# Gram with nine matmuls per group: low parts of the diagonal blocks in their lower triangles, rows divided by the diagonal, VectorE alone makes the diagonal block

## The chip, the cores and the metric

One NeuronCore of a Trainium2 chip runs the kernel. The time is the device time in microseconds (us) of one launch; the median of several executions counts. One more execution was profiled, and all rows below come from it.

## What is computed

For each of B=8 batches: S=112 query rows of width C=320, 20 heads of 16; a context of 375 rows of width 512, of which 371 (`text`) and 4 (`ip`) are attended apart. Cut to what matters:

```python
q = heads(x @ W_q); k_t = heads(text @ W_k); v_t = heads(text @ W_v)
probs_t  = softmax(q . k_t / 4)                       # over the 371 text rows
text_out = probs_t . v_t
qsem  = l2norm(probs_t . text)                        # 512 wide, for each head and query row
fused = q . k_ip / 4 + 0.5 * (qsem . l2norm(ip))      # 4 columns
out   = (text_out + softmax(fused) * mask . v_ip) @ W_out + b_out + x
```

The norm of `probs_t . text` is not taken from 512 wide vectors. With e the unnormalised probabilities and G = text . text^T (371x371, symmetric), its square is e^T G e. G is kept in two rounded parts, a high one (`Gh`) and the remainder (`Gl`), so that fast matmuls (type f32r) can use it.

## The kernel before

**Tiling.** The 371 text rows are three chunks (`ROWS`: 128, 128, 115). Heads go in groups of four: NG=5 groups per batch, g = 0 to 39 in all. For each group:

- `St` (S0, S1, S2, one per chunk): four matmuls of 112 columns into one of two PSUM banks `P`. ScalarE (ACT) takes the exponential into `big` (`eb`, line 681), then rounds it into `er` (line 685).
- `gram`, for j = 2, 1, 0: sums over i <= j of block (i, j) of G times chunk i of `er`, into one of two banks `Y`. Blocks above the diagonal carry a factor 2, so the upper triangle suffices. Each block takes two matmuls of 448 columns, one with `Gh` and one with `Gl`: 6 + 4 + 2 = 12. VectorE (DVE) multiplies each Y by `eb` (line 829) and GpSimd (POOL) adds the three products (line 547). `gram(g, 2)` waits for all three `er` of its group (`s_er`), and gram number y for the product of gram y-2 (`s_P`), since there are two banks `Y`.
- `pv` (v): 12 matmuls with V and 4 that add the products; ACT copies the result to `OT`.

**Preparation of a batch**, one batch ahead, shares three PSUM banks `PR` (the ring, NR=3): units `K` (keys: ACT rounds, DVE takes the rest), `G` (a block row of G, i = 0, 1, 2), `V`, 20 `max` (m: scores of one head, DVE reduces to the maximum, line 807), `mT` (transposes the maxima after the last m), and of the batch before `T`, `pT`, `cT`, `o`. A unit that writes ring bank n waits until the unit n-3 has been freed by its last reader (`freed`).

A unit `G` before: 12 matmuls into the bank; ACT copies the diagonal block to `Gh` (line 658), then twice the rest (line 661), then four columns to `Vt` (line 665); DVE writes both parts of `Gl` (lines 799, 801) and frees the bank.

**Order.** Each engine runs its instructions in the order of one list (`master_schedule`). For group g = 5b + r the words of `ROUNDS[r]` (batches 1 to 6), `EARLY[r]` (batch 0) or `LAST[r]` (batch 7) are written out one after the other. In them g stands for gram(g, 2), gram(g, 1), gram(g, 0); S0 to S2 for the St of group g+1; v for pv of group g-1; K, Kr for batch b+2; m, G, V, mT for batch b+1; T, r, pw, z, p, pT, cT, o for the end of batch b-1. ACT follows the list exactly; DVE follows it too, except that `behind()` lets some work wait until a later unit. `LATE` replaces the last round of batches 5 and 6.

Of the kernel before, what the change touches and what calls it, by code (L numbers as in the profile page):

```python
# [50 lines left out]
ROUNDS = ("S0 K0 m g m K1 S1 m v S2 m G0 m",  # L51
# [17 lines left out]
def master_schedule():  # L69
# [14 lines left out]
    order += [("G", 0, i) for i in range(3)] + [("K", 1, c) for c in range(3)] + [("Kr", 1)]  # L84
# [70 lines left out]
def build(nc, xT, xr, ctxT, ctxip, mask, wq, wk, wv, wkip, wvip, wout, bout, ident_d, hm_q, hm_v, krow, out):  # L155
# [13 lines left out]
    with ctx:  # L169
        def sb(name, shape, dt=f32):  # L170
            return ctx.enter_context(nc.sbuf_tensor(name, shape, dt))

# [16 lines left out]
        Gl = [sb(f"Gl{i}", [128, 768], f32r) for i in range(2)]  # L189
# [298 lines left out]
        def _(pool):  # L488
            fills = [0]

            def fill(region, value):
# [14 lines left out]
            fill(usel[:, 21:22], 1.0)  # L506
# [104 lines left out]
        def _(act):  # L611
# [3 lines left out]
            for u in order:  # L615
# [34 lines left out]
                elif k == "G":  # L650
                    b, i, r = u[1], u[2], ROWS[u[2]]
                    filled(act, u)
# [22 lines left out]
                elif k == "St":  # L675
# [9 lines left out]
                    act.activation(er[g % 2][:, 448 * c:448 * c + 448], e, ACT.Copy).then_inc(s_er, 1)  # L685
# [46 lines left out]
        def _(dve):  # L732
# [8 lines left out]
            for u in behind(order):  # L741
# [48 lines left out]
                elif k == "G":  # L790
                    b, i, r = u[1], u[2], ROWS[u[2]]
                    if b == 0:
                        dve.wait_ge(s_set, FILLS)
                    dve.wait_ge(s_gh, 3 * b + i + 1)
                    gh, gl = Gh[b % 2], Gl[b % 2]
                    a = min(128, T - 128 * i)
                    rest = T - 128 * i - a
                    o = GOFF[i]
                    low = dve.tensor_tensor(gl[0:r, o:o + a], bank[0:r, 0:a], gh[0:r, o:o + a].bitcast(f32), ALU.subtract)
                    if rest:  # L800
                        low = dve.scalar_tensor_tensor(gl[0:r, o + a:o + a + rest], bank[0:r, a:a + rest], 2.0,
                                                       gh[0:r, o + a:o + a + rest].bitcast(f32), ALU.mult, ALU.subtract)
# [100 lines left out]
        def _(pe):  # L903
# [6 lines left out]
            for u in order:  # L910
# [57 lines left out]
                elif k == "G":  # L968
# [8 lines left out]
                    last.then_inc(s_ring, 1)  # L977
                elif k == "V":
# [16 lines left out]
                elif k == "mT":  # L995
                    b = u[1]
                    if b == 0:
                        pe.wait_ge(s_w, 16 * FIRST)
# [18 lines left out]
                elif k == "gram":  # L1017
# [5 lines left out]
                    if j == 2 and r == 0:  # L1023
                        freed(pe, seq[("G", b, 2)])
# [149 lines left out]
```

## Time and profile before

| | |
|---|---|
| median of 3 executions | 411.6 us (411.37 to 414.6) |
| the profiled execution | 411.41 us, its span 409.6 us |
| TensorE (PE) matmuls | 393.6 us busy, 96% of the span |
| VectorE, ScalarE, GpSimd | 54%, 50%, 50% |

A row of a timeline gives start and duration in us, engine, line and operation, out<-in, shape and count, and in brackets how long the engine had been idle and who ended that. Durations of matmuls overlap: what a matmul costs the engine is the distance between two starts. PEld is the load of a matmul's weights. A row with x2 or more is several alike merged. Line numbers of these rows are those of the kernel before.

### The profile page before, as it was taken

The page shows a single profiled execution, that of the slowest core. Times are in us where ns is not written, and L with a number is a line of the kernel's source. Part 1 is how long each engine was busy: PE and PEld are TensorE (multiplying, and loading weights), DVE is VectorE, ACT ScalarE, POOL GpSimd, SP SyncE. Part 2 cuts the span into 40 slices and gives each one's busy share as a digit, 9 for nine tenths or more (in the row PEclk, how much of TensorE's full clock was granted, in tenths as well). Part 3 has the DMA queues.
Part 4 walks back from the last instruction along what each step waited for, and adds up shares of the span by engine and source line. Part 5 has one row for each costly group of instructions (what it writes and reads, how often), then busy time and mean ns, then how long its engine had stood idle before and what let it go on. Part 6 is the DMA issues. An engine that isn't in the chain of part 4 may idle for free.

```text
span 409.6 us, 9494 instructions
## 1 busy us (share of the span) xinstructions
PE 393.6 (96%) x3653; PEld 319.5 (78%) x3653; DVE 220.2 (54%) x482; ACT 206.0 (50%) x484; POOL 206.3 (50%) x218
## 2 busy tenths in 40 slices
PE   7999799899899999999999999999999999999995
PEld 4648688678788878888789878887888878876762
DVE  0795764575267534665366526663556646643432
ACT  1534134555645565555556564456455366458722
POOL 3020361262527872576437662687247443844981
PEclk9999999999999999999999999999999999999998
DMA  8499994338204802273207511470208210001000
GB/s 259 140 292 234 213 172 84 92 126 166 75 2 150 145 14 72 75 161 61 82 6 193 97 49 36 146 144 18 72 2 168 51 40 2 3 3 39 3 16 15
DMA packets 29455, 38.03 MB, mean 93 GB/s; under 512 B 14361, under 2 KB 26745, under 8 KB 28729
## 3 DMA queue, kind: packets, MB, share of 16 engines
q1 hardware_dynamic: 28514, 36.36, 37.0%
q10 hardware_dynamic: 896, 1.07, 0.9%
q8 instruction: 29, 0.48, 0.5%
q14 instruction: 16, 0.13, 0.1%
HBM read 28.50 MB, written 8.81 MB: 91 GB/s over the span
## 4 chain that ended last, share of the span: by engine, by line
PE 88%; DVE 3%; ACT 2%; issue 2%; DMA 2%; POOL 1%; POOLq 0%; SPq 0%; ACTq 0%; DVEq 0%
PE PR L905 42%; PE Y L905 27%; PE P L905 10%; PE O L905 8%; DMA pb<-wq 1%; DVE big L773 1%; PE PR L1063 1%; ACT big L681 1%; ACT er L685 1%; POOL pb L547 1%; DVE mx L807 1%; DMA qst<-ma 0%; POOLq L169 0%; SPq L460 0%; ACT cTs L729 0%
## 5 line engine op out<-in xcount | busy, mean ns | idle before, releaser
L547 POOL TENSOR_TENSOR pb<-pb 128x448 f32<-128x448 f32 x78 | 89.1, 1142 | 110.4 <-DVE pb L829 104.9
L807 DVE TENSOR_REDUCE mx<-PR 112x1 f32<-112x371 f32 x160 | 83.7, 540 | 78.1 <-PE PR L905 77.1
L905 PE MATMUL Y<-er,Gh 128*128 128x448 f32 x240 | 95.3, 397 | 1.7 <-ACT er L685 0.8
L829 DVE TENSOR_TENSOR pb<-big,Y 128x448 f32<-128x448 f32 x120 | 72.6, 621 | 39.2 <-PE Y L905 39.0
L905 PE MATMUL Y<-er,Gl 128*128 128x448 f32 x240 | 87.3, 364 | 0.0
L681 ACT ACTIVATE big<-P 128x448 f32<-128x448 f32 x120 | 65.2, 543 | 18.7 <-PE P L905 17.9
L685 ACT ACTIVATE er<-big 128x448 fp32r<-128x448 f32 x120 | 69.3, 578 | 3.8
L905 PEld LDWEIGHTS Y<-er,Gh 128*128 128x128 f32 x240 | 45.1, 188 | 13.7 <-DVE pb L829 9.1
L905 PE MATMUL PR<-kst,qst 96*112 96x371 bf16 x160 | 51.3, 331 | 2.2 <-DVE mx L807 2.0
L905 PEld LDWEIGHTS Y<-er,Gl 128*128 128x128 f32 x240 | 45.2, 188 | 2.1
L905 PE MATMUL P<-qst,kst 99*128 99x112 bf16 x480 | 42.0, 214 | 1.5 <-ACT big L681 1.1
L905 PEld LDWEIGHTS P<-qst,kst 99*128 99x128 bf16 x480 | 29.8, 99 | 17.0 <-issue 8.0
L649 ACT ACTIVATE ks<-PR 128x372 bf16<-128x372 f32 (+1 forms) x24 | 10.3, 429 | 47.8 <-PE PR L905 47.2
L905 PE MATMUL PR<-wvh,eh 128*128 128x320 f32 (+1 forms) x96 | 32.3, 336 | 0.2 <-ACT Vt L673 0.2
L673 ACT ACTIVATE Vt<-PR 128x320 f32<-128x320 f32 (+1 forms) x24 | 10.6, 442 | 41.2 <-PE PR L905 41.2
L905 PE MATMUL O<-big,Vt 128*22 128x112 f32 x960 | 31.0, 262 | 0.0
L905 PE MATMUL PR<-eh 128*128 128x376 f32 (+2 forms) x96 | 29.7, 310 | 0.0
L905 PE MATMUL PR<-wvl,eh 128*128 128x320 f32 (+1 forms) x96 | 29.7, 309 | 0.0
L905 PE MATMUL PR<-wvh,el 128*128 128x320 f32 (+1 forms) x96 | 29.6, 309 | 0.0
L569 POOL TENSOR_TENSOR t<-ssq,halfm 112x20 f32<-112x20 f32 (+2 forms) x9 | 28.8, 3202 | 1.4 <-DVE ssq L845 1.3
L905 PE MATMUL PR<-eh,el 128*128 128x376 f32 (+2 forms) x96 | 28.0, 292 | 0.0
L905 PE MATMUL PR<-el,eh 128*128 128x376 f32 (+2 forms) x96 | 28.0, 292 | 0.0
(154 smaller groups left out, 653.5 us busy)
## 6 DMA issues: line engine op xcount, KB each, us to landing
et<-ctxT SPq DMA_DIRECT2D x8, 752.0 KB, 4.4
kst<-kd SPq DMA_DIRECT2D x7, 720.0 KB, 7.2
kd<-ks SPq DMA_DIRECT2D x16, 288.0 KB, 2.9
qst<-qd SPq DMA_DIRECT2D x48, 70.0 KB, 2.4
kst<-kd SPq DMA_DIRECT2D x7, 480.0 KB, 9.9
kst<-kd SPq DMA_DIRECT2D x9, 240.0 KB, 9.0
qd<-kst SPq DMA_DIRECT2D x4, 336.0 KB, 5.6
vx<-xr SPq DMA_DIRECT2D x8, 140.0 KB, 2.2
```

The source lines that it names most:

```text
L547: pool.tensor_tensor(total, total, (pz, pm)[j], ALU.add).then_inc(s_S, 1)
L569: power = pool.tensor_tensor(t1[:, hs], ssq[:, hs], halfm[:, hs], ALU.pow)
L649: act.activation(ks[:, 0, TP * c:TP * c + w], bank[:, 0:w], ACT.Copy).then_inc(s_kh, 1)
L673: act.activation(Vt[b % 2][0:r, i, :, 0:D], bank[0:r, 0:C].rearrange("p (h d) -> p h d", d=D), ACT.Copy).then_inc(s_free[seq[u] % NR], 1)
L681: act.activation(e, P[(3 * g + c) % 2][:, 0:448], ACT.Exp).then_inc(s_exp, 1)
L685: act.activation(er[g % 2][:, 448 * c:448 * c + 448], e, ACT.Copy).then_inc(s_er, 1)
L773: dve.tensor_tensor(kblk[0:w, c, :, :].rearrange("p b (h n) -> p b h n", n=NIP), src, m, ALU.mult).then_inc(s_kb, 1)
L807: dve.tensor_reduce(mx[b % 2][:, h:h + 1], bank[0:S, 0:T], AX.X, ALU.max).then_inc(s_free[seq[u] % NR], 1)
L829: dve.tensor_tensor((pz, pm, pa[g % 2])[j], eb[g % 3][:, 448 * j:448 * j + 448], Y[y % 2][:, 0:448], ALU.mult).then_inc(s_P, 1)
L905: return pe.matmul(o, st, mv, start=start, stop=stop, **kw)
L1063: last = pe.transpose(bank[0:S, 128 * (r - lo):128 * (r - lo) + 128], OT[b % 2][:, r, :], ident[:, :])
```

## The change

- `er` is now the exponential times a number per text row (`gc`, the diagonal of G), rounded; the rows of G are divided by that number (`grc` its reciprocal) when they are copied. The diagonal of the divided block is exactly 1.
- The diagonal block of `Gh` holds, above the diagonal, the rounded values and half the diagonal; below it, the transposed low parts. So one matmul per diagonal block does what two did: gram takes 5 + 3 + 1 = 9 matmuls. The result is half of what it was; `usel` carries 2.0.
- DVE makes the diagonal block: six instructions per unit `G`, each waiting for the one before. ACT waits for the fifth (`s_gd`), then copies the rest and the `Vt` columns; DVE's part for the rest (`Gl`) comes as a held unit after the next max.
- A new ring unit `D` per block row: PE transposes the 128x128 low parts, and DVE adds them into `Gh`.
- The lists are rewritten: where G and D stand, and where m, K and V stand around them.

```diff
-ROUNDS = ("S0 K0 m g m K1 S1 m v S2 m G0 m",
-          "S0 m g m K2 m S1 v m S2 G1 m",
-          "S0 m g2 T0 T1 g1 g0 m r0 G2 m S1 m pw v S2 m V0",
-          "Kr S0 r1 m g m V1 m S1 m m v r2 S2 mT z V2",
+ROUNDS = ("S0 K0 m K1 m g m G0 S1 m v S2 m",
+          "S0 g m D0 m K2 m G1 S1 m v S2 m",
+          "S0 g2 T0 T1 g1 g0 m D1 r0 m G2 S1 m v S2 m pw",
+          "Kr S0 r1 g m D2 V0 m S1 m V1 m v r2 m S2 m mT z V2",
           "p E g pT v cT S0 S1 o S2")
 EARLY = ("m S0 m K1 g m S1 m S2 m",
-         "S0 m g m S1 K2 m S2 v m m",
-         "S0 m g m S1 m v S2 V0 m m",
-         "Kr S0 m g m V1 m S1 m m v S2 mT V2",
+         "S0 m D0 g m S1 K2 m S2 v m m",
+         "S0 m D1 g m S1 m v S2 V0 m m",
+         "Kr S0 m D2 g m V1 m S1 m m v S2 mT V2",
...
-    order += [("G", 0, i) for i in range(3)] + [("K", 1, c) for c in range(3)] + [("Kr", 1)]
+    order += [("G", 0, i) for i in range(3)]
+    order += [u for c in range(3) for u in (("K", 1, c), ("D", 0, c))] + [("Kr", 1)]
...
 ACT, unit G:
-                    filled(act, u)
+                    act.wait_ge(s_gd, 3 * b + i + 1)
...
-                    act.activation(Gh[b % 2][0:r, GOFF[i]:GOFF[i] + a], bank[0:r, 0:a], ACT.Copy)
-                    rest = T - 128 * i - a
+                    rest = T - 128 * i - r
                     if rest:
...
+                        act.activation(Gh[b % 2][0:r, GOFF[i] + r:GOFF[i] + r + rest], bank[0:r, r:r + rest],
+                                       ACT.Copy, scale=grc[b % 2][0:r, i:i + 1])
 ACT, unit St:
-                    act.activation(er[g % 2][:, 448 * c:448 * c + 448], e, ACT.Copy).then_inc(s_er, 1)
+                    act.activation(er[g % 2][:, 448 * c:448 * c + 448], e, ACT.Copy,
+                                   scale=gc[g // NG % 2][:, c:c + 1]).then_inc(s_er, 1)
 DVE, unit G:
+                    link(dve.scalar_tensor_tensor(low, bank[0:r, 0:r], 1.0, ident[0:r, 0:r], ALU.mult, ALU.mult, accum_out=c))
+                    link(dve.tensor_scalar(c, c, TINY, None, ALU.max))
+                    link(dve.reciprocal(rc, c))
+                    link(dve.scalar_tensor_tensor(diag, bank[0:r, 0:r], rc, half_upper[0:r, 0:r], ALU.mult, ALU.mult))
+                    dve.scalar_tensor_tensor(low, bank[0:r, 0:r], rc, diag.bitcast(f32), ALU.mult, ALU.subtract).then_inc(s_gd, 1)
+                    dve.wait_ge(s_gd, 3 * b + i + 1)
+                    dve.scalar_tensor_tensor(low, low, c, upper[0:r, 0:r], ALU.mult, ALU.mult).then_inc(s_ru, 1)
 DVE, units Gl and D (new):
+                        dve.scalar_tensor_tensor(Gl[b % 2][0:r, LOFF[i]:LOFF[i] + rest], PR[n % NR][0:r, r:r + rest],
+                                                 grc[b % 2][0:r, i:i + 1], Gh[b % 2][0:r, o + r:o + r + rest].bitcast(f32),
+                                                 ALU.mult, ALU.subtract).then_inc(s_free[n % NR], 1)
+                    dve.scalar_tensor_tensor(diag, bank[0:r, 0:r], grc[b % 2][0:r, i:i + 1], diag.bitcast(f32), ALU.mult,
+                                             ALU.add).then_inc(s_free[seq[u] % NR], 1)
 PE, units D (new) and gram:
+                    pe.wait_ge(s_ru, 3 * b + i + 1)
+                    pe.transpose(bank[0:r, 0:r], dj[i][0:r, 0:r], ident[0:r, 0:r]).then_inc(s_ring, 1)
...
-                        mm(d, Gh[b % 2][:, o:o + 128], mv, i == 0, False)
-                        last = mm(d, Gl[b % 2][:, o:o + 128], mv, False, i == j)
+                        last = mm(d, Gh[b % 2][:, o:o + 128], mv, i == 0, i == j)
+                        if i < j:
+                            o = LOFF[i] + 128 * (j - i - 1)
+                            mm(d, Gl[b % 2][:, o:o + 128], mv, False, False)
```

PE, from S2 of a round 0 (batch 2) to the first gram matmul of round 1. `P1<-qst2,kst2` is S2, `P0<-qst2,kst2` the next S0, `PR..<-kst0,qst0` a max, `PR2<-eh1`, `el1` the unit G0. Before:

```order
L905 MATMUL P1<-qst2,kst2 128x112 x4
L905 MATMUL PR1<-kst0,qst0 112x371
L905 MATMUL PR2<-eh1 128x376
L905 MATMUL PR2<-el1,eh1 128x376
L905 MATMUL PR2<-eh1,el1 128x376
...
L905 MATMUL PR0<-kst0,qst0 112x371
L905 MATMUL P0<-qst2,kst2 128x112 x4
L905 MATMUL PR1<-kst0,qst0 112x371
L905 MATMUL Y1<-er1,Gh0 128x448
```

and in the changed kernel, the end of G0 and what follows it:

```order
L941 MATMUL PR1<-eh1,el1 128x376
L941 MATMUL P0<-qst2,kst2 128x112 x4
L941 MATMUL PR2<-kst0,qst0 112x371
L941 MATMUL O<-big,Vt1 22x112 x12
L941 MATMUL O<-pb,usel 22x112 x4
L941 MATMUL P1<-qst2,kst2 128x112 x4
L941 MATMUL PR0<-kst0,qst0 112x371
L941 MATMUL P0<-qst2,kst2 128x112 x4
L941 MATMUL Y1<-er1,Gh0 128x448
```

G0 stood between S2 and the gram; it now stands ahead of S1, and one max and the next S0 are left between S2 and the gram. Rounds 1 and 2 changed in the same way around G1 and G2.

ACT, at the same place. `big<-P` is the exponential of an St, `er` its rounding, `Gh`, `Vt` the copies of unit G. Before:

```order
L681 ACTIVATE big<-P0 128x448
L685 ACTIVATE er1<-big 128x448
L693 ACTIVATE OT1<-O 128x112
L681 ACTIVATE big<-P1 128x448
L685 ACTIVATE er1<-big 128x448
L658 ACTIVATE Gh1<-PR2 128x128
L661 ACTIVATE Gh1<-PR2 128x243
L665 ACTIVATE Vt1<-PR2 128x20x4
```

and in the changed kernel:

```order
L676 ACTIVATE Gh1<-PR1,grc1 128x243
L680 ACTIVATE Vt1<-PR1 128x20x4
L696 ACTIVATE big<-P0 128x448
L700 ACTIVATE er1<-big,gc0 128x448
L709 ACTIVATE OT1<-O 128x112
L696 ACTIVATE big<-P1 128x448
L700 ACTIVATE er1<-big,gc0 128x448
```

G's copies stood behind the er of S2; they now stand ahead of the exponential of S1.

PE, behind the gram of a round 1 (the last two gram matmuls, then max, D0, max, K2, whose first matmul is the last row). Before:

```order
L905 MATMUL Y1<-er1,Gh0 128x448
L905 MATMUL Y1<-er1,Gl0 128x448
L905 MATMUL PR2<-kst0,qst0 112x371
L905 MATMUL PR0<-et,wk2 64x186 x8
L905 MATMUL PR1<-kst0,qst0 112x371
```

and in the changed kernel:

```order
L941 MATMUL Y1<-er1,Gh0 128x448
L941 MATMUL PR1<-kst0,qst0 112x371
L1019 MATMUL PR2<-masks,dj0 128x128
L941 MATMUL PR0<-kst0,qst0 112x371
L941 MATMUL PR1<-et,wk2 64x186 x8
```

The unit three places behind the first max was a max behind K2; it is now K2 itself, with only D0 and one max between.

## Rows read from the trace of the kernel before

**Rows 1.** The page: busy time of PE; the chain that ended last, by engine.

```profile
PE 393.6 (96%) x3653; PEld 319.5 (78%) x3653; DVE 220.2 (54%) x482; ACT 206.0 (50%) x484; POOL 206.3 (50%) x218
...
PE 88%; DVE 3%; ACT 2%; issue 2%; DMA 2%; POOL 1%; POOLq 0%; SPq 0%; ACTq 0%; DVEq 0%
```

**Rows 2.** Windows: stretch, length, busy us of PE, PEld, DVE, ACT, POOL, then PEclk.

```profile
120.00:320.00 200.00, 199.23 (x1964) 168.57 (x1962) 109.84 (x246) 108.16 (x257) 118.55 (x115) 1.00 0.38 89
...
402.00:406.00 4.00, 3.14 (x10) 1.12 (x10) 1.58 (x8) 1.33 (x5) 0.76 (x1) 1.00 0.00 0
```

**Rows 3.** Timeline, PE: last matmuls of a gram (g = 11) and the max behind it.

```profile
211.38 0.36 PE L905 MATMUL Y<-er,Gl 128*128 128x448 f32 x1
211.66 0.47 PE L905 MATMUL Y<-er,Gh 128*128 128x448 f32 x1
211.97 0.36 PE L905 MATMUL Y<-er,Gl 128*128 128x448 f32 x1
212.17 0.32 PE L905 MATMUL PR<-kst,qst 96*112 96x371 bf16 x1
```

**Rows 4.** Timeline, PE: S1; S2 behind max and pv; max, S0, max behind G0.

```profile
205.21 0.37 PE L905 MATMUL P<-qst,kst 99*128 99x112 bf16 x4
...
206.57 0.37 PE L905 MATMUL P<-qst,kst 99*128 99x112 bf16 x4
...
209.05 0.32 PE L905 MATMUL PR<-kst,qst 96*112 96x371 bf16 x1
209.21 0.36 PE L905 MATMUL P<-qst,kst 99*128 99x112 bf16 x4
209.41 0.32 PE L905 MATMUL PR<-kst,qst 96*112 96x371 bf16 x1
```

**Rows 5.** Timeline, ACT: the same stretch.

```profile
206.35 0.58 ACT L685 ACTIVATE er<-big 128x448 fp32r<-128x448 f32 x1
206.84 0.24 ACT L693 ACTIVATE OT<-O 128x112 f32<-128x112 f32 x1
206.98 0.54 ACT L681 ACTIVATE big<-P 128x448 f32<-128x448 f32 x1
...
209.43 0.37 ACT L661 ACTIVATE Gh<-PR 128x243 fp32r<-128x243 f32 x1
...
209.80 0.57 ACT L681 ACTIVATE big<-P 128x448 f32<-128x448 f32 x1
210.40 0.58 ACT L685 ACTIVATE er<-big 128x448 fp32r<-128x448 f32 x1
```

**Rows 6.** Timeline, batch 0: an S2, its er, the gram that waits for it.

```profile
79.09 0.37 PE L905 MATMUL P<-qst,kst 99*128 99x112 bf16 x4
...
80.10 0.58 ACT L685 ACTIVATE er<-big 128x448 fp32r<-128x448 f32 x1
...
80.83 0.44 PE L905 MATMUL Y<-er,Gh 128*128 128x448 f32 x1 [0.84 <-ACT er L685]
```

**Rows 7.** Timeline, DVE: two small instructions, the second waiting for the first.

```profile
404.25 0.20 DVE L860 RECIPROCAL zm<-zm 112x8 f32<-112x8 f32 x1
404.49 0.23 DVE L861 TENSOR_SCALAR zm<-zm,mask_s 112x8 f32<-112x8 f32 x1
```

**Rows 8.** Timeline, DVE: the maximum of the max that PE starts at 212.17.

```profile
212.91 0.54 DVE L807 TENSOR_REDUCE mx<-PR 112x1 f32<-112x371 f32 x1
```

**Rows 9.** Timeline, PE: transposes of 128 columns.

```profile
174.14 0.71 PE L1063 MATMUL PR<-ident,OT 128*112 128x128 f32 x5
```

**Rows 10.** Timeline: the two places before group 0 with three units G together.

```profile
37.51 0.28 DVE L799 TENSOR_TENSOR Gl<-PR,Gh 128x128 fp32r<-128x128 f32 x1
...
38.45 0.39 PE L905 MATMUL PR<-eh,wkh 128*128 128x372 f32 x1
...
66.26 0.28 ACT L658 ACTIVATE Gh<-PR 128x128 fp32r<-128x128 f32 x1 [3.12 <-PE PR L905]
...
69.42 0.54 ACT L681 ACTIVATE big<-P 128x448 f32<-128x448 f32 x1 [0.21 <-PE P L905]
```

More of the change, by code:

```diff
@@ L21 @@
 GOFF = (0, 384, 640)
+LOFF = (0, 256)
+TINY = 1e-30
 STACK = ((0, 3), (1, 2), (2, 1))
-FILLS = 17
-FIRST, REST = 2, 6
+FILLS = 19
+FIRST, REST = 1, 6
 HH = 10
@@ L101, in master_schedule @@
                 unit.update({"G0": ("G", n, 0), "G1": ("G", n, 1), "G2": ("G", n, 2)})
+            if n < B:
+                unit.update({"D0": ("D", n, 0), "D1": ("D", n, 1), "D2": ("D", n, 2)})
             if n + 1 < B:
@@ L135, in behind @@
     for u in order:
-        if u[0] in ("K", "G") and u[1] >= 2:
+        if u[0] == "K" and u[1] >= 2:
             out, held = out + held, [u]
+        elif u[0] == "G":
+            out, held = out + held + [u], [("Gl",) + u[1:]]
         else:
             out.append(u)
-            if u[0] in ("max", "gram", "mT", "o"):
+            if u[0] in ("max", "gram", "mT", "o", "K"):
                 out, held = out + held, []
     return out + held
-RING = ("K", "G", "V", "T", "pT", "cT", "o", "max", "mT")
+RING = ("K", "G", "D", "V", "T", "pT", "cT", "o", "max", "mT")
 NR = 3
@@ L188, in build @@
         Gh = [sb(f"Gh{i}", [128, 768], f32r) for i in range(2)]
-        Gl = [sb(f"Gl{i}", [128, 768], f32r) for i in range(2)]
+        Gl = [sb(f"Gl{i}", [128, 384], f32r) for i in range(2)]
+        gc = [sb(f"gc{i}", [128, 3]) for i in range(2)]
+        grc = [sb(f"grc{i}", [128, 3]) for i in range(2)]
+        dj = [sb(f"dj{i}", [128, 128]) for i in range(3)]
         Vt = [sb(f"Vt{i}", [128, 3, H, MV]) for i in range(2)]
@@ L225, in build @@
         res = [sb(f"res{i}", [S, C]) for i in range(2)]
+        ident, half_upper, upper = [masks[:, 128 * i:128 * i + 128] for i in range(3)]
         vrT = et[:, 0, 0:H * NIP * 3].rearrange("p (c n) -> p c n", c=3)
@@ L256, in build @@
         s_w2 = sem("s_w2")
+        s_mk = sem("s_mk")
         s_pw = sem("s_pw")
@@ L287, in build @@
         s_pad = sem("s_pad")
+        s_gd = sem("s_gd")
         s_gh = sem("s_gh")
+        s_ru = sem("s_ru")
         s_ms = sem("s_ms")
@@ L505, in _ @@
             fill(usel[:, :], 0.0)
-            fill(usel[:, 21:22], 1.0)
+            fill(usel[:, 21:22], 2.0)
+            for i in range(2):
+                fill(gc[i][:, :], 1.0)
             fill(half[:, :], 0.5)
@@ L977, in _ @@
                     last.then_inc(s_ring, 1)
+                elif k == "D":
+                    b, i, r = u[1], u[2], ROWS[u[2]]
+                    pe.wait_ge(s_ru, 3 * b + i + 1)
+                    if b == 0 and i == 0:
+                        pe.wait_ge(s_mk, 16)
+                    pe.transpose(bank[0:r, 0:r], dj[i][0:r, 0:r], ident[0:r, 0:r]).then_inc(s_ring, 1)
                 elif k == "V":
@@ L1023, in _ @@
                     if j == 2 and r == 0:
-                        freed(pe, seq[("G", b, 2)])
+                        for i in range(3):
+                            freed(pe, seq[("D", b, i)])
                     if j == 2:
@@ L1163 @@
         "bout": np.ascontiguousarray(L0_xattn_b_out),
-        "ident_d": np.eye(128, dtype=np.float32),
+        "ident_d": np.concatenate([np.eye(128), np.triu(np.ones((128, 128)), 1) + np.eye(128) / 2,
+                                   np.triu(np.ones((128, 128)), 1)], 1).astype(np.float32),
         "hm_q": np.ascontiguousarray(hm_q),
```

33 lines of the change are left out of this document (20 added, 13 removed).

## The prediction

> **What bounds the kernel now.** I read the page first. TensorE is busy for 96% of the span and makes 88% of the chain of work that ended last [rows 1]; from 120 to 320 us it is busy for 199.2 of 200 us [rows 2]. Matmul durations overlap, so I went by the distance between starts. A gram matmul costs 0.20 us (211.97 to 212.17) [rows 3]. Steady batches run with PE nearly gapless. So work taken from PE shortens the kernel, but only while nothing that PE waits for becomes late. I therefore read next, in the timeline, how long the others need from a trigger on PE to the thing PE wants back, and compared it with the work that stands between the two in PE's order, now and in the change.
>
> **What the change removes.** Three of twelve matmuls in each of 40 groups: 120 x 0.20 = 24.0 us.
>
> **What gram gives back at once.** gram j=0 waits for DVE's product of j=2, with only the matmuls of j=1 to cover it. Now this costs 0.28 - 0.20 = 0.08 us in the start (211.38 to 211.66) and 0.11 more behind it (0.31 to the next instead of 0.20) [rows 3]. The cover shrinks from four matmuls to three, so the wait grows by one matmul, 0.20 us. That holds for the 29 groups whose list says g (5 in batch 0, 24 in batches 1 to 6), and about for four groups of the last batch: 33 x 0.20 = 6.6 us.
>
> **D on PE.** Five transposes together last 0.71 us [rows 9], so one costs at most 0.14 us: 24 x 0.14 = 3.4 us.
>
> **ACT behind the diagonal chain: the largest term.** gram(g, 2) needs the er of its group's S2. In batch 0 there is one place where almost nothing stands between: S2 starts at 79.09, its er at 80.10, gram at 80.83, after PE had idled 0.84 us [rows 6]. So S2 to gram takes 1.74 us with ACT free. In the steady rounds before, S2 to the max ahead of gram is 206.57 to 209.41 = 2.84 us, since G0 (or G1, V) stood between [rows 4]. In the new rounds 0, 1 and 2 only a max and the next S0 follow S2: 0.20 + 0.16 + 0.20 = 0.56 us of PE work [rows 4]. That alone leaves PE 1.74 - 0.56 = 1.18 us idle. And ACT won't be free: in its order the copies of G stand ahead of S1's exponential, and they now wait for DVE.
>
> Take 0 as the end of G0's slots on PE. Its bank is full at +0.20 (a matmul ends 0.16 after the next may start [rows 3], plus 0.04 to hand over). DVE then runs five instructions, each waiting for the one before: two like the 128x128 subtraction of 0.28 [rows 10], reading PSUM, a maximum and a reciprocal on one column, and another 128x128. Dependent small ones stand 0.24 apart at 0.20 each, so 0.04 is the handover [rows 7]. That is 3 x 0.29 + 2 x 0.20 + 4 x 0.03 = 1.39 us. The trace has no instruction with an accumulator output: it may cost nothing, or one more small instruction (0.24); I take nothing. From below the chain is 1.27 (no handovers), from above 1.39 + 0.24 + 0.2 (small ones as long as the second of rows 7, wider ones slower) = 1.83. ACT starts at +1.65. From there its distances are the measured ones [rows 5]: copy to exponential 0.37 (209.43 to 209.80), exponential to er 0.60, er to OT 0.49, OT to exponential 0.14, exponential to er again 0.60, so S2's er starts at +3.85; from start of er to gram is 0.73 (80.10 to 80.83) [rows 6]: gram at +4.58. PE meanwhile has S1, max, pv (1.36, 205.21 to 206.57), S2, max, S0 (0.56) [rows 4] = 1.92 us. **PE idles 2.66 us.** Around G1 the copy is shorter by 0.10: 2.56. Around G2 there is no rest to copy and the block is 115 wide: 2.36. Per batch 7.58, in six batches 45.5 us. Queued behind ACT's wait are the exponentials of S1 and S2, for which PE's next S0 and the gram wait; nothing on PE can step ahead, since it runs in order.
>
> The scale of er is a column of numbers now; whether this costs ACT anything no row shows. I take nothing, and for the upper end 0.1 us in each of eight such instructions on the way (two er and mostly a copy per stall): 4.8 us.
>
> The Trainium skill ("ScalarE: Activation LUTs", section "What ACT_TABLE_LOAD costs") says that each pointer operand of an ACTIVATE adds about 93 ns. By it the sum below would be 8 x 6 x 0.093 = 4.5 us higher (an estimate from that page); the trace of before has no such ACTIVATE.
>
> **The ring.** A unit waits until the one three places ahead is freed. Behind the gram of round 1 stand max, D0, max, K2; K2 waits for the first max. PE starts a max at 212.17, DVE reaches it at 212.91 because it multiplies products first, and frees it 0.54 later [rows 3, 8]: 1.28 + 0.06 = 1.34 us. PE has 0.16 + 0.14 + 0.16 = 0.46 us of work: 0.88 idle. Round 2 has max, D1, max, G2 behind g1 g0, where with g1 and g0 next to each other both products still lie ahead of DVE (I take 0.4 us more, two matmuls less of head start): 1.29. In round 3 mT now follows a max at once and waits for it: three maxima in a row at 0.5 apart with S2 between, 0.9. Together 3.07, in six batches 18.4 us. Twice in batch 0 D waits 0.3: 0.6 us. From below all of this could be nothing, if DVE frees sooner.
>
> **Before group 0.** Two places have three units G together. DVE takes them strictly in turn: chain 1.39, ACT 0.05 + 0.5, Gl 0.44, so about 2.4, 2.3, then 1.4 to the third's release. At the second place the bank is full at 66.26 and the first exponential ran at 69.42 [rows 10]; now it can't before 66.26 + 2.4 + 2.3 + 1.4 + 0.1 = 72.5, and the ring holds K: I take 2.5 us (of up to 3.1). At the first place DVE starts at 37.51 and K at 38.45 [rows 10]; K now waits to 37.5 + 2.4 = 39.9 (1.4), the next K for the third G (2.8 more): 4.2. Together 6.7, from below nothing.
>
> **Sum.** -24.0 + 6.6 + 3.4 + 45.5 + 18.4 + 0.6 + 6.7 = +57.2. On the profiled execution's 411.4 this gives 468.6; the median is 0.2 higher: **469 us**. The extra DVE work (about 1.4 us per G, 34 us in all, on an engine busy 54%) costs nothing beyond the chain. If only the ring term falls away the time is 450; with the chain at 1.83 (18 x 0.44 = 8) and er dearer (4.8) it is 482; a few waits of the V copies that I left out add 2 or 3. Own range: 446 to 488.
>
> **Rivals.**
> - *The chain doesn't hold ACT* (ACT finds the diagonal done, or the copies overlap): each stall is only the 1.18 us of S2 to gram. 18 x 1.18 = 21.2 instead of 45.5: 444 us. For it: rows 6 show that figure; against it: the chain is bounded from below by 1.27 us.
> - *Faster:* PE's work decides, as it does now [rows 1, 2], and the stalls don't come: -24.0 + 6.6 + 3.4 = -14.0, 397 us. It needs er(S2) within 0.56 us of S2, or stalls and ring waits below 14.0 / 18 = 0.78 us per round. Rows 6 show 1.74, so I hold little of it. The Trainium skill ("Perfetto Trace Analysis", "Identifying Performance Opportunities") speaks for this one: it says that improving a kernel means improving its most contended engine, here PE, which the change relieves.
> - *No change:* the stalls come to about 14 us by luck: 411 us.
> - *The clock falls:* PE now idles 2.5 us at a time. Where it already idles some 0.9 us in 4, the granted clock stayed at 1.00 [rows 2], its level of 2.4 GHz; longer gaps no row shows. If PE ran half of the 6.3 us it streams per stalled round at 1.2 GHz, that is 3.1 x 18 = 56 us more: about 525 us. The Trainium skill ("TensorE: Matmul & The Clock Gate", "What's actually happening") says that the throttled state is the default, and activity releases it.
>
> **How the numbers follow.** Forecast 0.72; chain doesn't hold ACT 0.12; clock 0.07; faster 0.06; no change 0.03. Forecast and first rival together fill 442 to 490, with a little cut off each end. Faster by over 1% 0.06, within 1% (about what a measurement of this kernel can tell) 0.03, slower by over 1% 0.91.
>
> **What would show it.** In steady batches, three gram matmuls per batch with 2.4 to 2.7 us idle before them, released by er; the ACT copy of G waiting for DVE's fifth instruction, 1.4 us after the first; K2, G2 and mT waiting for a maximum by 0.9 to 1.3 us; PE busy near 80% of the span with its clock at 1.00; gram matmuls still 0.20 apart; a steady batch longer by 7.6 + 3.1 - 3.0 + 0.8 + 0.4 = 8.9 us. The prediction is wrong if gram's idle time in these rounds is below 1 us, if the DVE chain takes under 1 us, or if the clock drops.

## The result and the profile after

| | before | after |
|---|---|---|
| median | 412.2 us (4 runs, 411.4 to 414.6) | 501.7 us (4 runs, 500.6 to 503.7) |
| ratio | | 1.217 (1.210 to 1.223) |
| span of the profiled execution | 409.6 us | 499.1 us |
| mean granted clock of TensorE | 0.997 | 0.934 |
| a steady batch, from one transpose of the maxima (mT) to the next, mean of four | 44.6 us | 58.2 us |

The kernel is 89.6 us slower. Forecast was 57 slower, and the time lies above the range. The page of the changed kernel: busy time, the clock in 40 slices, the chain that ended last.

```profile
PE 413.6 (83%) x3557; PEld 322.6 (65%) x3557; DVE 259.5 (52%) x650; ACT 210.1 (42%) x460; POOL 205.9 (41%) x220
...
PEclk9998998999878998889988998889969998999998
...
PE 56%; DVE 17%; ACT 10%; issue 9%; POOL 4%; DMA 2%; SPq 1%; POOLq 0%; ACTq 0%; DVEq 0%
```

Against [rows 1] PE fell from 96 to 83% busy, and DVE and ACT entered the chain. PE is busy for longer although it has 96 matmuls less: the clock row dips all through the kernel. The waits (engine and what it waited for: us in total, times, longest):

```profile
ACT Gh L676 <- DVE dj L820: 68.8, 16, 7.4
ACT Vt L680 <- DVE dj L820: 33.5, 8, 5.2
PE Y L941 <- ACT er L700: 31.3, 20, 1.7
PE P L941 <- ACT big L696: 17.5, 22, 1.5
PEld PR L941 <- DVE mx L843: 16.8, 15, 1.4
PEld Y L941 <- DVE pb L865: 14.3, 32, 1.4
PE PR L1043 <- DVE mx L843: 5.7, 7, 0.8
```

These are the waits that the prediction named: ACT stands for DVE's fifth instruction, gram for er, K2, G2 and mT for a maximum. The fourth row is the next S0, which waits for the exponential of S1, since that frees its bank P; it was named too. A steady round 0, first DVE's chain for one G, then ACT behind it:

```profile
186.42 0.29 DVE L816 SCALAR_TENSOR_TENSOR dj<-PR,masks 128x128 f32<-128x128 f32 x1 [1.23 <-PE PR L941]
186.63 0.08 DVE L816 DVE_READ_ACCUMULATOR dj<-PR,masks 128x1 f32 x1
186.75 0.15 DVE L817 TENSOR_SCALAR gc<-gc 128x1 f32<-128x1 f32 x1
186.94 0.16 DVE L818 RECIPROCAL grc<-gc 128x1 f32<-128x1 f32 x1
187.14 0.35 DVE L819 SCALAR_TENSOR_TENSOR Gh<-PR,grc,masks 128x128 fp32r<-128x128 f32 x1
187.53 0.35 DVE L820 SCALAR_TENSOR_TENSOR dj<-PR,grc,Gh 128x128 f32<-128x128 f32 x1
```

```profile
187.91 0.46 ACT L676 ACTIVATE Gh<-PR,grc 128x243 fp32r<-128x243 f32 x1 [5.89 <-DVE dj L820]
188.27 0.23 ACT L680 ACTIVATE Vt<-PR 128x80 f32<-128x80 f32 x1
188.39 0.55 ACT L696 ACTIVATE big<-P 128x448 f32<-128x448 f32 x1
188.97 0.67 ACT L700 ACTIVATE er<-big,gc 128x448 fp32r<-128x448 f32 x1
...
190.25 0.67 ACT L700 ACTIVATE er<-big,gc 128x448 fp32r<-128x448 f32 x1
```

and PE: S2, max, the next S0, then gram(g, 2):

```profile
187.51 0.37 PE L941 MATMUL P<-qst,kst 99*128 99x112 bf16 x4
187.71 0.32 PE L941 MATMUL PR<-kst,qst 96*112 96x371 bf16 x1
188.99 0.37 PE L941 MATMUL P<-qst,kst 99*128 99x112 bf16 x4 [0.95 <-ACT big L696]
191.06 0.71 PE L941 MATMUL Y<-er,Gh 128*128 128x448 f32 x1 [1.70 <-ACT er L700]
191.57 0.57 PE L941 MATMUL Y<-er,Gl 128*128 128x448 f32 x1
191.95 0.57 PE L941 MATMUL Y<-er,Gh 128*128 128x448 f32 x1
```

PE is idle for 0.95 + 1.70 = 2.65 us; by starts it is (1.28 - 0.16) + (2.07 - 0.20) = 2.99. Behind it the gram matmuls start 0.37 to 0.38 apart instead of 0.20. Windows of the same place (stretch, length, PE busy, granted clock, DMA) say why:

```profile
190.00:191.00 1.00, 0.00 (x0) 0.98 0.00 0
191.00:192.00 1.00, 0.94 (x3) 0.50 0.06 16
192.00:193.00 1.00, 1.00 (x4) 0.50 0.00 0
...
194.00:195.00 1.00, 1.00 (x6) 0.81 0.00 0
```

At the end of the stall the clock falls from 1.00 to 0.50, its level of 1.2 GHz, for some 3 us of dense work. The stalls of the next two rounds do the same (0.50 again from 205 to 208 and from 215 to 218 us). But not every stall does. Taken in windows of 1 us, the clock fell after 13 of the 18, and stayed at 1.00 after those that end at 273.75, 380.69, 390.59, 431.64 and 441.54 us. The first of these five, with the next matmul close behind:

```profile
273.75 0.44 PE L941 MATMUL Y<-er,Gh 128*128 128x448 f32 x1 [1.70 <-ACT er L700]
274.03 0.37 PE L941 MATMUL Y<-er,Gl 128*128 128x448 f32 x1
```

Over the whole span, 499.1 x (1 - 0.934) = 33 us of clock is lost, against 1 before.

### The profile page after: what moved, and what is told of

The parts are those of the page before. It is cut to its first block, busy times and chain, and to the rows that moved or that the text cites. A ratio compares the mean times of both kernels' runs of the same rounds, so it can differ in the third digit from the quotient of the medians.

```text
span 499.1 us, 9507 instructions
## 1 busy us (share of the span) xinstructions
PE 413.6 (83%) x3557; PEld 322.6 (65%) x3557; DVE 259.5 (52%) x650; ACT 210.1 (42%) x460; POOL 205.9 (41%) x220
## 3 DMA queue, kind: packets, MB, share of 16 engines
q10 hardware_dynamic: 896, 1.07, 0.7%
## 4 chain that ended last, share of the span: by engine, by line
PE 56%; DVE 17%; ACT 10%; issue 9%; POOL 4%; DMA 2%; SPq 1%; POOLq 0%; ACTq 0%; DVEq 0%
PE PR L941 32%; PE Y L941 15%; DVE pb L865 4%; ACT big L696 4%; PE P L941 4%; DVE mx L843 3%; ACT er L700 3%; PE O L941 3%; DMA et<-ctxT 2%; DVE Gh L819 2%; DVE dj L820 2%; POOL pb L564 2%; DVE dj L816 1%; POOL t L586 1%; PE PR L1109 1%
## 5 line engine op out<-in xcount | busy, mean ns | idle before, releaser
L941 PE MATMUL Y<-er,Gh 128*128 128x448 f32 x240 | 98.3, 444 | 35.4 <-ACT er L700 31.3
L865 DVE TENSOR_TENSOR pb<-big,Y 128x448 f32<-128x448 f32 x120 | 71.5, 619 | 90.8 <-PE Y L941 88.7
L843 DVE TENSOR_REDUCE mx<-PR 112x1 f32<-112x371 f32 x160 | 82.5, 536 | 53.2 <-PE PR L941 52.9
L941 PEld LDWEIGHTS Y<-er,Gh 128*128 128x128 f32 x240 | 53.1, 221 | 52.8 <-issue 34.4
L700 ACT ACTIVATE er<-big,gc 128x448 fp32r<-128x448 f32 x120 | 80.3, 669 | 3.9
L941 PE MATMUL P<-qst,kst 99*128 99x112 bf16 x480 | 42.2, 214 | 18.4 <-ACT big L696 17.5
L941 PE MATMUL PR<-kst,qst 96*112 96x371 bf16 x160 | 52.5, 341 | 2.5 <-DVE mx L843 2.4
L941 PEld LDWEIGHTS P<-qst,kst 99*128 99x128 bf16 x480 | 27.4, 98 | 36.1 <-ACT big L696 23.4
L941 PE MATMUL Y<-er,Gl 128*128 128x448 f32 x120 | 50.4, 420 | 0.0
L676 ACT ACTIVATE Gh<-PR,grc 128x243 fp32r<-128x243 f32 (+1 forms) x16 | 6.6, 410 | 68.8 <-DVE dj L820 68.8
L941 PE MATMUL PR<-eh 128*128 128x376 f32 (+2 forms) x96 | 30.8, 321 | 5.4 <-DVE mx L843 5.4
```

The source lines that it names most:

```text
L676: act.activation(Gh[b % 2][0:r, GOFF[i] + r:GOFF[i] + r + rest], bank[0:r, r:r + rest], ACT.Copy, scale=grc[b % 2][0:r, i:i + 1])
L843: dve.tensor_reduce(mx[b % 2][:, h:h + 1], bank[0:S, 0:T], AX.X, ALU.max).then_inc(s_free[seq[u] % NR], 1)
L865: dve.tensor_tensor((pz, pm, pa[g % 2])[j], eb[g % 3][:, 448 * j:448 * j + 448], Y[y % 2][:, 0:448], ALU.mult).then_inc(s_P, 1)
L941: return pe.matmul(o, st, mv, start=start, stop=stop, **kw)
```

## The experiments

"Clock lost" is the span times one minus the mean granted clock, of the profiled execution. Batch is the steady batch as above.

| kernel | median us | ratio to before | clock lost | batch |
|---|---|---|---|---|
| after | 501.7 | 1.217 (1.210 to 1.223) | 32.9 | 58.2 |
| e1 order alone | 453.3 | 1.097 (1.091 to 1.102) | 8.5 | 51.0 |
| e2 8 idle matmuls | 481.2 | 1.164 (1.157 to 1.170) | 10.1 | 54.6 |
| e2b 4 idle matmuls | 482.0 | 1.166 (1.161 to 1.171) | 8.2 | 54.9 |
| e3 copies late | 451.4 | 1.092 (1.087 to 1.098) | 4.9 | 49.9 |
| e4 old lists | 438.4 | 1.061 (1.056 to 1.067) | 9.2 | 47.6 |
| e5 e3 and ring | 447.8 | 1.085 (1.080 to 1.090) | 4.5 | 49.3 |
| e6 er by a constant | 495.2 | 1.198 (1.194 to 1.202) | 29.1 | 57.3 |
| e7 new lists | 423.2 | 1.025 (1.020 to 1.030) | 7.1 | 44.0 |
| e8 and batch 0 | 417.3 | 1.011 (1.002 to 1.019) | 2.1 | 44.0 |
| e9 and nip moved | 416.2 | 1.006 (1.004 to 1.009) | 4.1 | 44.0 |
| e10 and start | 418.5 | 1.014 (1.011 to 1.017) | 7.1 | 44.0 |

**e1: the order alone, without the new arithmetic.** The kernel before, with the new `ROUNDS` less their D. Here and in the diffs below `...` marks a cut.

```diff
-ROUNDS = ("S0 K0 m g m K1 S1 m v S2 m G0 m",
-          "S0 m g m K2 m S1 v m S2 G1 m",
+ROUNDS = ("S0 K0 m K1 m g m G0 S1 m v S2 m",
+          "S0 g m m K2 m G1 S1 m v S2 m",
...
```

> The kernel before with the changed kernel's ROUNDS (without the D units), arithmetic as before: twelve matmuls per gram, no chain on VectorE. Theory (the places in the list are a cause by themselves): S2 to gram(g,2) takes 1.74 us with ScalarE free and the list leaves 0.56 us of work between, so TensorE idles about 1.2 us in rounds 1, 2 and 3 of six batches (21 us), and the ring waits of K2, G2 and mT (0.9, 1.3, 0.9) stay (18 us): 411.6 + 39 = about 451 us, if the granted clock stays at 1.00. If gaps of 1.2 us already make the clock fall, 1.5 us more for each of 18: about 478 us, mean clock near 0.94. Rival (the chain on VectorE is the whole cause): within 5 us of 412.

453.3 us, near the 451 that the theory gave. Twelve matmuls, ACT making the diagonal block, and still 41 us slower: gram waits for er 19 times.

```profile
PE Y L905 <- ACT er L685: 22.1, 19, 1.5
```

So nearly half of the loss is there before DVE's chain enters: too little work stands between S2 and gram, and between a maximum and the unit that takes its bank. The clock fell after 3 of the 18 stalls (1.52 us long; it stayed after three others of 1.52, and after all those of 1.05 and 0.97).

**e2 and e2b: keep PE awake.** The changed kernel with idle matmuls (results unused) ahead of gram(g, 2)'s wait in rounds 1 to 3 of batches 1 to 6. They are 448 columns wide, 0.20 us each; the 128 in the text of e2b is wrong.

```diff
+                    if j == 2 and 1 <= b < B - 1 and 1 <= r <= 3:
+                        for _ in range(FILL):
+                            mm(d, Gh[b % 2][:, 0:128], Gh[b % 2][:, 0:448], True, True)
                     if j == 2:
                         pe.wait_ge(s_er, 3 * g + 3)
```

> The changed kernel with eight more matmuls of 448 columns (Gh times Gh, into the bank Y that gram overwrites, so the output is the same) ahead of the wait for er in rounds 1, 2, 3 of batches 1 to 6: 144 matmuls more, in the 1.7 us in which TensorE idles. Theory (the part of the loss that the prediction missed is the clock, which falls to 0.50 after each of these 18 stalls and costs about 1.6 us each): mean granted clock 0.99 or more, gram matmuls 0.20 us apart behind the wait, time 501.7 - 29 = about 473 us (468 to 478). Rival (the miss is longer waits, the low clock only goes along): no gain, or slower by the added work, 500 to 510 us.

> e2_filler with 4 idle products of 128 columns instead of 8 ahead of the gram product that waits for er; the products go nowhere, the computation is complete. Theory (the clock falls after long idle stretches of TensorE; e3's of 1.1 us left it at 1.00, the changed kernel's of 1.7 behind 1.2 did not): 4 fill some 0.25 us or more of the 1.7, which is between the two: about 481 us if the clock then stays as in e2_filler, about 500 us if it falls as in the changed kernel.

481.2 and 482.0 us. Matmuls that compute nothing make the kernel 20.6 us faster. They stand where PE would have idled, and what they buy is the clock: 200 us of steady batches, after, with 8 and with 4 of them (PEclk is the number behind the five engines):

```profile
150.00:350.00 200.00, 163.44 (x1492) 132.61 (x1492) 99.33 (x257) 85.05 (x187) 92.52 (x91) 0.92 0.27 63
```

```profile
150.00:350.00 200.00, 179.63 (x1668) 144.97 (x1666) 105.23 (x271) 90.87 (x198) 95.61 (x93) 1.00 0.29 68
```

```profile
150.00:350.00 200.00, 172.97 (x1623) 138.13 (x1622) 104.29 (x268) 89.99 (x196) 95.09 (x93) 0.99 0.28 66
```

The clock fell after none of the 18 stalls with eight, and after two of them with four (0.58 from 143 to 147 and 0.57 from 188 to 192 us). Filling about half of the 1.7 us (with 0.8 still waited for er) serves nearly as well as filling all. The waits of S0 for ACT are the same in e2 as after (17.5 us, 22 times). This prices the clock: 20.6 us by the medians, 32.9 - 10.1 = 23 by the clock itself, and a batch of 58.2 against 54.6.

**e3: ACT doesn't wait for the chain.** ACT's copies of G, from batch 2 on, stand behind the er of S2 in ACT's list; PE and DVE are as after. The new function, cut to what matters:

```diff
+        if u[0] == "G" and 2 <= u[1]:
+            held = [u]
+        else:
+            out.append(u)
+            if u[0] == "St" and u[2] == 2:
+                out, held = out + held, []
```

> The changed kernel, only ScalarE's order changed: its copies of G (from batch 2 on) stand behind the er of S2 instead of ahead of S1's exponential, so that no exponential waits for VectorE's chain. Theory: the wait of the next S0 (0.6 to 0.9 us and more) goes, and gram's wait shrinks to that of S2's er, about 1.3 us with an er of 0.67; stalls of 2.9 us become 1.3 us: 18 x 1.6 = 29 us less, 473 us if the clock still falls after each, 445 us with a mean clock of 0.99 if it doesn't. Rival (ScalarE's wait for the chain is not on the path): 495 to 503 us.

451.4 us, 50 less. S2 and the gram of the same round, with what it still waits:

```profile
187.09 0.37 PE L954 MATMUL P<-qst,kst 99*128 99x112 bf16 x4
...
188.89 0.45 PE L954 MATMUL Y<-er,Gh 128*128 128x448 f32 x1 [1.07 <-ACT er L713]
189.17 0.36 PE L954 MATMUL Y<-er,Gl 128*128 128x448 f32 x1
```

S2 to gram is 187.09 to 188.89 = 1.80 us, near the 1.74 that the prediction took from [rows 6]. The matmuls behind stay 0.2 apart: none of the 18 stalls of 1.07 us was followed by a lower clock. Against e2 (481.2 us, the clock back and the waits kept) e3 is 29.8 us shorter, and the theory had 29 for the waiting; the other 20.6 of the 50 us are the clock, as e2 priced it. So the branch of the theory in which the clock no longer falls (445 us) is the one that came, 6 us too low. Its stalls were to be 1.3 us; they are 1.07 by the bracket and 1.23 by starts (187.46 for S0, 188.89 for gram).

**e4: the new arithmetic in the old order.** Before's lists, with D put in.

```diff
+ROUNDS = ("S0 K0 m g m K1 S1 m v S2 m G0 m",
+          "S0 m g m D0 K2 m S1 v m S2 G1 m",
+          "S0 m g2 T0 T1 g1 g0 m D1 r0 G2 m S1 m pw v S2 m V0",
+          "Kr S0 r1 m g m D2 V1 m S1 m m v r2 S2 mT z V2",
...
```

> The changed kernel's arithmetic (nine matmuls, chain on VectorE, D) with the lists of before for batches 1 to 6, the D units put in behind the gram of rounds 1 and 3 and behind the max of round 2. Theory: G0, G1 and V stand between S2 and gram again, so er is never late, the clock stays at 1.00, and what is left is 24.0 us saved against 6.6 (gram j=0), 3 (D), 6 to 7 before group 0, and waits of T0 for G1's bank, about 1 us in six batches: 400 to 412 us. Rival (the arithmetic itself is what costs, wherever it stands): over 440 us.

438.4 us: 63 us won, but neither the 400 to 412 expected nor over 440, though close under the rival's bound. er is in time now; other waits took its place, the longest for DVE's products.

```profile
PEld Y L941 <- DVE pb L865: 26.4, 32, 2.2
PE Y L941 <- DVE pb L865: 12.9, 12, 1.8
```

G stands next ahead of gram in these lists, so its chain and its Gl lie in DVE's order ahead of the products that gram's own last part waits for: the chain starts at 175.74, Gl at 178.07, the products at 178.90. Once a batch gram waits 1.7 to 1.8 us for them, and T 1.2 us for the bank of G1, which the theory had named. After three of the six long waits for the products the clock fell. One of them:

```profile
179.56 0.47 PE L941 MATMUL Y<-er,Gh 128*128 128x448 f32 x1 [1.80 <-DVE pb L865]
```

**e5: free the ring.** e3, with other work between the maxima and K2, G2 and mT.

```diff
-          "S0 g m D0 m K2 m G1 S1 m v S2 m",
+          "S0 g m D0 K2 m m G1 S1 m v S2 m",
...
```

> e3_copies_late (451.42 us) with the lists of rounds 1 to 3 written so that at least one product or S2 stands between each D or G and the r, K or V that takes the next of the ring of tiles. Theory (the ring term): the waits for VectorE's max before K2 (0.9 to 1.3 us), G2 (1.3) and mT (0.9), some 3 us a batch in six batches, go: 18 us less, about 433 us. Rival (the waits only uncover another wait behind them, on er or on the block's factor): 448 us or more.

447.8 us, only 3.6 less, with intervals that overlap; the rival held. In a timeline of PE, K2 waits no more (0.73 us in e3), but G1, three places behind it, waits 0.79 us for K2's own bank. G2 waits no more either (1.07 in e3), but the third max behind it does, for G2's bank:

```profile
197.19 0.36 PE L954 MATMUL PR<-kst,qst 96*112 96x371 bf16 x1 [1.52 <-DVEq L846]
```

DVE frees that bank (line 846) only behind ACT's copies of G2, which e3 had moved behind the er of S2. So the wait for a maximum went, and another wait for a bank of the ring came, with the units three places behind the moved ones.

**e6: the price of the column.** er's scale is a constant; the multiplication of er by `gc` is left out.

```diff
-                                   scale=gc[g // NG % 2][:, c:c + 1]).then_inc(s_er, 1)
+                    act.activation(er[g % 2][:, 448 * c:448 * c + 448], e, ACT.Copy).then_inc(s_er, 1)
```

> The changed kernel with a constant in place of the column gc as scale of the activation that writes er, so the multiplication of er by gc is left out. Theory (the column costs 0.09 us an activation, 669 against 577 ns in the two traces, and counts where ScalarE is what TensorE waits for, twice a round in 18 rounds): 2 x 0.09 x 18 = 3.3 us less, 498.5 us. Rival (the row difference comes from something else, or ScalarE's time there is hidden): no change, 501.7 us.

495.2 us, 6.6 less instead of 3.3. er of the changed kernel and of e6 in the groups of instructions (busy us, mean ns):

```profile
L700 ACT ACTIVATE er<-big,gc 128x448 fp32r<-128x448 f32 x120 | 80.3, 669 | 3.9
```

```profile
L700 ACT ACTIVATE er<-big 128x448 fp32r<-128x448 f32 x120 | 69.3, 577 | 3.8
```

92 ns an instruction. The wait of gram for er is 1.52 us here instead of 1.70, and 18 x 0.18 = 3.2 us is what the theory had. The rest goes with the clock (32.9 - 29.1 = 3.8 us lost less): here it fell after 14 of the 18 stalls, for the same 3 us each time; in the changed kernel after 13, but from 133 to 140 and from 365 to 376 us it stayed low two and three times as long. Whether the shorter stalls have a part in that isn't shown.

**e7: lists for this arithmetic.** A K or V stands between S2 and gram, every G a round ahead, a max between g2 and g1, and ACT's copies behind the next S.

```diff
+ROUNDS = ("S0 K0 m m g2 m g1 g0 S1 m v m G0 S2 K1 m",
+          "S0 m g2 m g1 g0 D0 S1 m v m G1 S2 K2 m",
+          "S0 g2 T0 T1 g1 g0 m D1 r0 S1 m pw v m G2 S2 V0 m",
+          "Kr S0 r1 m g2 m g1 g0 D2 V1 m S1 m m v r2 S2 mT z V2",
...
```

> The arithmetic with nine matmuls a group, complete, with ScalarE's copies of a block held behind the next S's exponential, lists in which a K or V product stands between S2 and the gram product of the same round, every G a round ahead of the group that uses it, and other products between the gram products of one group. Theory (all the loss is of order, and the nine matmuls save 120 x 0.20 = 24 us of TensorE): 393 to 400 us, the granted clock at 1.00 in the steady batches. Rival (VectorE's chain of six small instructions for a block costs TensorE time wherever it stands): 425 us or more.

423.2 us: 78.5 us of the 89.6 came back by order alone, with the arithmetic untouched, though not the 393 to 400 expected, and with little left to the rival's 425. The same place as above (end of G, S2, first matmul of K1; its last, max, S0, max, gram):

```profile
217.80 0.34 PE L953 MATMUL PR<-eh,el 128*128 128x376 f32 x1
217.97 0.37 PE L953 MATMUL P<-qst,kst 99*128 99x112 bf16 x4
218.16 0.42 PE L953 MATMUL PR<-eh,wkh 128*128 128x372 f32 x1
...
220.13 0.34 PE L953 MATMUL PR<-eh,wkl 128*128 128x372 f32 x1
220.30 0.32 PE L953 MATMUL PR<-kst,qst 96*112 96x371 bf16 x1
220.46 0.36 PE L953 MATMUL P<-qst,kst 99*128 99x112 bf16 x4
220.90 0.36 PE L953 MATMUL PR<-kst,qst 96*112 96x371 bf16 x1
221.00 0.47 PE L953 MATMUL Y<-er,Gh 128*128 128x448 f32 x1
```

No wait: 2.14 us of K1 cover er and the chain, which takes as long as ever (218.25 to 219.71 on DVE). A batch is 44.0 us, 0.6 less than before. The nine matmuls promised 3.0. In the timelines of one batch each, the starts of the gram matmuls span 13.4 us for 60 before and 11.4 for 45 here, so 2.0 is the true gain; a gram matmul that follows another unit takes 0.3 instead of 0.2, and splitting a group into pieces makes more of these. D (0.4) and short waits around S and max take back about 1 more. The other loss lies in batch 0 and the next, where clock falls follow waits.

**e8, e9, e10: batch 0.** e8 puts D behind the group's products; e9 moves three instructions of DVE on `nip` (2.25 us, once) to a calmer place; e10 puts K and G ahead of the first S.

```diff
-         "S0 m D0 g m S1 K2 m S2 v G2 m m",
+         "S0 m g D0 m S1 m K2 v S2 G2 m",
...
+                    if u == ("max", 1, 19):
+                        dve.tensor_scalar(nip[:, :], nip[:, :], EPS, None, ALU.max).then_inc(s_nip, 1)
...
-    order += [("mT", 0), ("G", 1, 0)] + [("St", 0, 0), ("St", 0, 1), ("K", 2, 0), ("St", 0, 2)]
+    order += [("mT", 0), ("G", 1, 0), ("K", 2, 0), ("G", 1, 1)] + [("St", 0, c) for c in range(3)]
```

> e7_new_lists with the lists of batch 0 changed so that the products of a group stand ahead of the D that needs VectorE's chain, and a pv product stands between K2 and the G behind it. In e7 TensorE stood 2.12 us ahead of a D at 85.6 us and 1.52 us ahead of a max product at 94.7 us, and the granted clock was 0.50 from 95 to 98 us behind it. Theory (these waits are of order): 2.1 + 1.5 us of waiting and some 1.5 us of low clock go, about 418 us. Rival (the chain moves the wait to the next product): 422 us or more.

> e8_early with VectorE's three instructions on nip (2.25 us in a row, once) moved from between the products of group 7 to behind the last max of batch 1. In e7 they stood ahead of a max for which TensorE waited 1.73 us at 142.0 us, and the granted clock was 0.50 from 143 to 149 us. Theory (this single delay starts the fall of the clock): 1.7 us of waiting and 3.5 us of low clock go against e8, about 413 us. Rival (something else makes the clock fall there): as e8.

> e9_early_nip with the first K product of batch 2 and the second G of batch 1 moved ahead of the first S, where TensorE stood 2.77 us for the DMA of the maxima and the granted clock was 0.50 from 71 to 77 us. Theory (that wait is covered by 3.4 us of products, and the fall of the clock behind it goes too): 2.8 us of waiting and some 3 us of low clock less than e9's 416.2, about 411 us, 2 us below before. Rival (the ring of tiles holds the moved products back, or the DMA's wait isn't shortened): 414 us or more.

417.3 (expected 418), 416.2 (expected 413; the rival, as e8, held) and 418.5 us (expected 411; the rival's 414 or more held). In e9 the wait at 142 us is gone, and so is the fall of the clock there. But in e8's profile that same wait was there, and the clock stayed. The wait in e7 and the window behind it (stretch, length, PE busy, granted clock), then the same of e8:

```profile
142.04 0.36 PE L953 MATMUL PR<-kst,qst 96*112 96x371 bf16 x1 [1.73 <-DVE mx L855]
...
144.00:148.00 4.00, 4.00 (x19) 0.50 0.84 154
```

```profile
139.71 0.36 PE L953 MATMUL PR<-kst,qst 96*112 96x371 bf16 x1 [1.74 <-DVE mx L855]
...
138.00:148.00 10.00, 8.29 (x59) 1.00 0.84 174
```

So a single stall of 1.7 us doesn't decide it, and what sets it stays open. The order of the program doesn't decide it either: of four launches of e8 two had a mean clock of 0.995 and 0.999 (415.5 and 414.4 us) and two of 0.983 (419.2 and 419.9 us). In e10 the wait for the DMA of the maxima went as planned, but the first S2 then stood behind an ACT that waited for the chain of the second G, the very pattern of the change:

```profile
78.01 0.36 ACT L688 ACTIVATE Gh<-PR,grc 128x115 fp32r<-128x115 f32 x1 [2.60 <-DVE dj L832]
```

```profile
78.98 0.55 PE L953 MATMUL P<-qst,kst 99*128 99x112 bf16 x4 [2.65 <-ACT big L708]
```

No version beat the kernel before: the best, e9, is 0.6% slower (0.4 to 0.9).

## Why the prediction was right and wrong

**Right: the mechanism and its places.** All three stalled rounds, ACT held by the chain, K2, G2 and mT held by a maximum, each in the row that was named. The rival "faster" fails on [rows 6], as said: gram needs 1.7 to 1.8 us from S2. The rule of the Trainium skill that stood beside it ("Perfetto Trace Analysis", "Identifying Performance Opportunities"), to improve the most contended engine, doesn't hold by itself here: PE was relieved of 24 us of matmuls, and the order took 78.5 (e7).

**The terms, one by one.**
- *The stall behind the chain*, forecast 2.66 us, was 2.99 by starts in round 0. DVE starts 0.27 behind the end of G0's slots (forecast 0.20), and its chain to ACT took 187.91 - 186.42 = 1.49 (forecast 1.45). The rest is the column as scale, taken as nothing: from the copy to the exponential 0.48 instead of 0.37, from the first er to OT 0.57 instead of 0.49, from the second er to gram 0.81 instead of 0.73. In rounds 1 and 2 the stall is 2.88 and 2.60 (forecast 2.56 and 2.36).
- *The Trainium skill*, "ScalarE: Activation LUTs", section "What ACT_TABLE_LOAD costs", had the column right: about 93 ns for a pointer operand; the trace agrees with 92 (577 to 669 ns). The column belonged in the sum. e6, without the one on er, is 6.6 us shorter, 3.2 of them by the shorter waits.
- *The accumulator output* is a row of its own, DVE_READ_ACCUMULATOR, 0.08 long; the next instruction starts 0.33 behind the start of the first. Two instructions of the same width without one stand 0.39 apart (187.14 to 187.53), so the 0 that was taken, from bounds of 0 and 0.24, fits.
- *The ring.* K2 1.02, G2 0.83 and mT 0.82 us (brackets in the timeline of PE), 2.67 together, where 0.88, 1.29 and 0.9 were forecast, 3.07. The size was fair. That it is a cost of its own that other lists in the round would give back is not: e5 won 3.6 us.
- *gram j=0*: 14.3 us of waits for the products (32 times), against 9.1 us (30 times) among the waits of the kernel before: 5 more where 6.6 was forecast.
- *Before group 0*: 5.5 us to the first mT (69.40 against 63.89 us), forecast 4.2 for that part, and 9.9 to the first gram matmul (85.23 against 75.34), forecast 6.7; the clock fell twice on the way (from 44 and from 81 us).
- With the clock held at 1.00 a steady batch is 54.6 us (e2), 10.0 more than before, forecast 8.9. In six batches that is 7 to 8 us of the miss; the longer stalls above make up 0.9 of the 1.1.

**Wrong: the clock.** The sum ran every matmul at 0.20, and "the clock falls" stood beside it as a rival of 0.07, at 56 us on top. What failed is that step, twice. First its chance: the rows showed at 1.00 only 0.86 us of idle time in 4 [rows 2], in two gaps of 0.42 and 0.44 us, the forecast itself made gaps of 2.6, and no row spoke for the clock staying there. (The trace of before has one longer gap, 1.84 us ahead of a max at 50.64 us, and the clock stayed; in e1 it fell after the same gap.) Second its size: one half of 6.3 us in every stalled round was assumed, 3.1 us each; e2 shows 20.6 us over 18 rounds, 1.1 each, since the clock fell after 13 of the 18 and mostly for 3 us. A drop of the clock was among the prediction's own signs of being wrong. So the miss of 32.4 us is about 20 of clock, 8 of longer stalls in the six batches, and 4 at the two ends, which no run took apart. (From the second mT to the last: before 259.4, after 340.8, e2 320.4 us; the forecast was 53.4 more than before.) (501.7 - 32.9 = 468.8 meets the forecast partly by luck: not all lost clock is lost time.) The range ended at 488 because the rival stood outside it, instead of its price being carried into the forecast's own upper end.

The clock's row in the windows above goes from 0.98 to 0.50 behind the stall. The Trainium skill, "TensorE: Matmul & The Clock Gate", section "What's actually happening", has the throttled state as the default that activity releases; the trace agrees, with 0.50 from 191 to 194 us and 1.00 again from 195, behind dense matmuls.

**What stays open.** Which pattern of idle time makes the clock fall. Of the 18 stalls of a kernel it fell after none with 1.07 us (e3), after 2 with 0.8 behind four idle matmuls (e2b), after 13 with 0.57 to 0.96 and then 1.70 (after), after 14 with 1.52 in place of 1.70 (e6); of six lone stalls after 3 with 1.7 to 1.8 (e4) and 3 with 1.52 (e1), but after none of six of 1.52 in e5. Equal stalls in one launch went both ways, so their length alone doesn't decide it. Order alone costs 41 us (e1), the arithmetic in the old order 26 (e4), both 89.6: the 22 us that are in neither come with the two together. That they are about the size of the clock that e2 gave back doesn't show that they are the same; e3 took off 50 us by parting the two on ACT alone.

## What to carry to other kernels

Before matmuls are saved on a saturated TensorE, list for each of its waits the work that stands between trigger and wait, and see that a long unit still stands there; here 0.56 us instead of 2.84, with the shorter ways round the ring, cost 41 us (e1), and 120 matmuls gave 24 at most. Where an in-order engine is to wait for another one's chain, put what the bounding engine needs ahead of that wait (e3: 50 us by moving three copies in one list). A stall of 1.5 us or more in every round should be priced with the clock in the forecast itself, and as a chance for each stall: here the clock fell after 13 of 18 (1.70 us), and after none of 18 of 1.07.

## What the runs showed of the hardware

- Idle matmuls ahead of a wait shorten the time (e2: 501.7 to 481.2 us), as the clock stays at 1.00.
- The same stall (1.70 us for er) is followed by 0.50 for some 3 us in one batch and by 1.00 in another of the same launch (13 of 18 and 5 of 18, after). Two launches of one kernel can differ in it: mean clock 0.999 and 0.983, 414.4 and 419.9 us (e8).
- At a granted clock of 0.50 a gram matmul of 448 columns starts 0.37 us behind the last, at 1.00 0.20.
- A column as scale costs an activation of 128x448 92 ns (669 against 577).
- Dependent DVE instructions stand 0.38 to 0.39 apart for 128x128 and 0.19 for one column; an accumulator output shows as a row of 0.08, and the next instruction starts 0.33 behind the first, no later than without one.
